# Storing each part of the last project tile once, and copying the rest during the scan

## What is computed

```python
xn = layernorm(layernorm(x)) * ln_w + ln_b
xi, z = split(xn @ W_in)                      # 512 channels each
u = silu(causal_conv(xi, 4 taps) + conv_b)
dt, Bm, Cm = split(u @ W_xproj)               # 16, 64, 64
delta = softplus(dt @ W_dt + b_dt)
for t in range(2048):                         # for each sequence, h is 512 x 64
    h = h * exp(delta[t] * A) + (delta[t] * u[t]) * Bm[t]
    y[t] = sum(h * Cm[t], over the 64 states)
out = x + layernorm(x) + ((y + u * D) * silu(z)) @ W_out
out = out + ffn(layernorm(out))               # silu(gate) * up, down
```

## Time and profile before

| what | us |
|---|---|
| median of 3 runs (lowest to highest) | 5815.9 (5814.91 to 5816.22) |
| the profiled execution | 5813.2 |
| its span | 5811.4 |
| VectorE busy in the span | 5505.2 (95%) |
| TensorE busy | 5241.6 (90%) |
| ScalarE busy | 3494.6 (60%) |
| GpSimd busy | 2262.3 (39%) |

### The profile page before, as it was taken

The page is one execution under the profiler, slowest core; times in us unless marked ns, Lnnn a source line. Parts: engine busy times, 40 slices in busy tenths (PEclk is TensorE's granted clock), DMA queues, the critical chain, the costliest instruction groups (busy, mean ns, idle before and its releaser), DMA issues. The chain is left out here.

```text
span 5811.4 us, 149606 instructions
## 1 busy us (share of the span) xinstructions
PE 5241.6 (90%) x38780; PEld 2478.7 (43%) x38780; DVE 5505.2 (95%) x3555; ACT 3494.6 (60%) x8238; POOL 2262.3 (39%) x6777
## 2 busy tenths in 40 slices
PE   5999779999999999999999999999999999997999
PEld 3344334444444444444444444444444444435666
DVE  5999989999999999999999999999999999995776
ACT  6777656666666666666666666666666666652333
POOL 2000034444444444444444444444444444440111
PEclk9999889999999999999999999999999999998999
DMA  7999942222222222222222222222222222224342
GB/s 245 332 321 337 344 111 53 54 54 55 54 52 53 54 54 54 54 52 53 54 54 55 54 52 53 54 55 54 54 52 54 53 55 54 54 44 147 115 141 73
DMA packets 1105518, 547.25 MB, mean 94 GB/s; under 512 B 753744, under 2 KB 1015056, under 8 KB 1105056
## 3 DMA queue, kind: packets, MB, share of 16 engines
q1 hardware_dynamic: 1093776, 533.89, 34.4%
q10 hardware_dynamic: 11664, 12.52, 0.6%
HBM read 296.83 MB, written 249.82 MB: 94 GB/s over the span
## 5 line engine op out<-in xcount | busy, mean ns | idle before, releaser
L997 DVE TENSOR_TENSOR_SCAN s_h<-s_decay,s_ubank 128x1024 f32<-128x1024 f32 x2048 | 4460.9, 2272 | 11.5 <-ACT s_ubank L962 11.2
L949 ACT ACTIVATE s_decay<-s_abank 128x512 f32<-128x512 f32 x4096 | 2210.4, 595 | 4.8 <-PE s_abank L887 1.4
L872 PE MATMUL s_ybank<-s_h,s_window 128*8 128x256 f32 x16416 | 1948.2, 602 | 1.9 <-DVE s_h L997 1.9
L913 PE MATMUL s_ubank<-s_x,s_w 128*128 128x256 bf16 x8192 | 1245.7, 275 | 375.5 <-DVE s_h L997 375.3
L1033 POOL TENSOR_TENSOR s_carry<-s_decay,s_h 128x64 f32<-128x64 f32 x2032 | 879.5, 433 | 1752.2 <-ACT s_decay L949 1576.4
L962 ACT ACTIVATE s_ubank<-s_seed 128x64 f32<-128x64 f32 x2048 | 478.3, 234 | 1703.2 <-PE s_ubank L913 1311.6
L887 PE MATMUL s_abank<-xnT,s_a 128*128 128x256 bf16 x8192 | 1254.9, 274 | 33.2 <-DMA s_w<-scratch_b_rows 30.1
L913 PEld LDWEIGHTS s_ubank<-s_x,s_w 128*128 128x128 bf16 x8192 | 675.7, 98 | 1197.7 <-DVE s_h L997 1096.5
L887 PEld LDWEIGHTS s_abank<-xnT,s_a 128*128 128x128 bf16 x8192 | 758.4, 98 | 195.8 <-ACT s_decay L949 35.7
L872 PEld LDWEIGHTS s_ybank<-s_h,s_window 128*8 128x8 f32 x16416 | 376.9, 97 | 839.6 <-issue 730.6
L1037 POOL TENSOR_TENSOR s_seed<-s_carry,s_first 128x64 f32<-128x64 f32 x2048 | 656.7, 321 | 164.3 <-ACT s_first L955 4.0
(11 more groups left out here) (135 smaller groups left out, 3098.2 us busy)
## 6 DMA issues: line engine op xcount, KB each, us to landing
s_x<-scratch_u_rows SPq DMA_DIRECT2D x4096, 32.0 KB
scratch_u_rows<-p_u_turn SPq DMA_DIRECT2D x90, 1024.0 KB, 6.6
scratch_delta_rows<-p_dparts SPq DMA_DIRECT2D x136, 512.0 KB, 6.2
xnT<-scratch_delta_rows SPq DMA_DIRECT2D x1024, 64.0 KB, 2.7
scratch_y<-s_y SPq DMA_DIRECT2D x1036, 16.0 KB
scratch_sz<-p_sz SPq DMA_DIRECT2D x16, 1024.0 KB, 6.2
scratch_u<-p_u SPq DMA_DIRECT2D x16, 1024.0 KB, 7.9
s_w<-scratch_b_rows SPq DMA_DIRECT2D x256, 64.0 KB, 2.4
```

The source lines that it names most:

```text
L872: last = nc.tensor.matmul(y_bank[32 * ct:32 * ct + WIN, 1 - x, :], window[:, of, (at + t) * WIN:(at + t + 1) * WIN], H[:, 1 - x, :, t], st ...
L913: last = nc.tensor.matmul(dst.rearrange("p q (a t) -> p a q t", t=2), w2[:, g, 4 * s + 2 * x + e, :], x2[:, s, :, 2 * x + e, q:q + 32, :], ...
L949: nc.scalar.activation(dst.rearrange("p x q t -> p q x t"), a_bank[:, b].rearrange("p j r (x t) -> p (j r) x t", x=2), ACT.Exp).then_inc(e ...
L997: nc.vector.tensor_tensor_scan(H[:, x, PT * p:PT * p + PT, :].rearrange("p q t -> p (q t)"), decay[:, x * (1 + c % 2), p].rearrange("p q t ...
```

## The change

In the project stage's tail, the last delta stores are cut from eight to three, one for each part, and the last u stores from five to three; the numbers that SyncE waits for are adapted. The first of COMBOS' entries, 0 to 2, are those that stay. The seven missing rows, five of delta (512 KB each) and two of u (1024 KB each), are copied from HBM to HBM by SyncE in the scan stage: one after each of the first seven groups of four chunks. For this SyncE's first 28 chunks are written out as straight code in place of loop iterations; the rest of the loop is in two pieces, from chunk 28 to 239 and from 240, and between them SyncE waits for the seven copies. Chunk 240 is the first that reads the rows of the last tile. The other engines' code is the same.

```diff
-            def back_stores(i, c, b):
+            def back_stores(i, c, b, stored=NCB):
                 sp.wait_ge(d3_done, i + 1)
-                for k, (_, j) in reversed(list(enumerate(COMBOS))):
+                for k, (_, j) in reversed(list(enumerate(COMBOS[:stored]))):
                     sp.dma_start(tile_of(d["delta_rows"][k], i), dparts[:, j]).then_inc(dparts_stored, 16)
...
-                        if j == part and k < PLACES:
+                        if j == part and k < (PARTS if last_one else PLACES):
...
             turn_stores(NT)
-            back_stores(NT, 0, BATCH)
+            back_stores(NT, 0, BATCH, PARTS)
             turn_stores(NT + 1, True)
...
-            sp.wait_ge(dparts_stored, 16 * NCB * (NT + 1))
+            sp.wait_ge(dparts_stored, 16 * (NCB * NT + PARTS))
...
-                sp.wait_ge(turns_stored[j], 16 * COPIES[j] * (NT + 3))
+                sp.wait_ge(turns_stored[j], 16 * (COPIES[j] * (NT + 2) + 1))
...
+N_COPIES = NCB - PARTS + PLACES - PARTS
+
+
+def copy_rows(eng, d, i, n, done):
+
+    if n < NCB - PARTS:
+        cols = slice(i * TW + TW, i * TW + 2 * TW)
+        eng.dma_start(d["delta_rows"][PARTS + n][:, cols], d["delta_rows"][n % PARTS][:, cols]).then_inc(done, 16)
+    else:
+        k = n - (NCB - PARTS)
+        rows = slice(i * TW + 2 * TW, i * TW + 3 * TW)
+        eng.dma_start(d["u_rows"][rows, PARTS + k, :], d["u_rows"][rows, k, :]).then_inc(done, 16)
...
-            over_chunks(sp, chunk)
+            for it in range(N_COPIES):
+                for c in range(4):
+                    chunk(it, it * 4 + c, c)
+                copy_rows(sp, d, NT - 1, it, copied)
+            last_tile = NF // 4 - NF // NT // 4
+            with sp.Fori(N_COPIES, last_tile) as it:
+                for c in range(4):
+                    chunk(it, it * 4 + c, c)
+            sp.wait_ge(copied, 16 * N_COPIES)
+            with sp.Fori(last_tile, NF // 4) as it:
+                for c in range(4):
+                    chunk(it, it * 4 + c, c)
```

More of the change, by code:

```diff
@@ L787, in scan_stage @@
         y_stored = [sem("y_stored0"), sem("y_stored1")]
+        copied = sem("s_copied")
         block = ctx.enter_context(nc.Block())
```

## The result

The changed kernel takes 5953.7 us (5948.5 to 5956.8, 6 runs) against 5815.95 us before (5814.15 to 5816.22): a ratio of 1.0238, with a 95% interval of 1.0228 to 1.0249. Forecast was 5805.0. The change is 138 us slower, not 11 us faster.

What follows compares the result with a forecast made beforehand. VectorE's scan instruction was taken to bound the scan stage, and the drain of stores to end the project stage. Gains of 9.0 + 1.9 - 0 = 10.9 us gave a forecast of 5805.0 us, range 5802.8 to 5808.5.

Steps and rivals of the forecast that it cites:

- term 3: Scan stage: the seven copies cost 0 us, since a copy may hold SyncE's load queue about 11 us before VectorE waits.
- nothing from writing out: Rival: late code fetches or transfer-bound issue in SyncE's straight chunks remove the 1.9 us gain; 5806.9 us, chance 0.13.
- with nothing to spare: Scan loop: the last x2 load's issue ends at 900.87 us and its data are used at 902.58 us.
- Term 1: Project stage's end: with fewer stores to drain, VectorE's xnT memset ends the stage; 9.0 us gained (8.8 to 9.1).
- Term 2: Scan stage's opening: written-out chunks drop SyncE's address instructions, about 0.14 us a load, plus loop entry; 1.9 us gained (0.5 to 2.3).
- the copies stop the scan: Slow-side rival: copies through one DMA engine hold up later loads, five stalls of 14 us, two of 39; 5953 us, chance 0.05.

Runs made afterwards that it cites:

- the straight run: The changed kernel with all 256 of SyncE's chunks written out and no loop at all: 5802.6 us, ratio 0.9980.
- the padded kernel: The changed kernel plus 80 no-effect SyncE instructions behind the project stage's last store and 48 between the loop's two pieces: 5806.4 us, ratio 0.9988.
- the last run: The changed kernel, all SyncE chunks written out, xnT's clearing shared by VectorE and GpSimd, which starts after VectorE's last split: 5800.8 us, ratio 0.9976.

## Why the prediction was wrong

The step that failed is the last sentence of term 3: "After the seventh copy the old loop runs with its old margins." It treats the code behind the written-out chunks as unchanged, because its instructions are. Its place is not. The sum has no term for that, and no rival had it: "nothing from writing out" looks for late fetches in the straight code, where the straight run shows none in 256 chunks, and uses the Trainium skill's rule only where it favours straight code. "Runtime: NRT & Kernel Launch" of the Trainium skill, section on instruction fetch mechanics, also says that a taken branch whose target isn't in the current window forces a fetch before execution can go on. The loop of the kernel before jumps back 63 times without the gap, which I read as that not applying here; with 32 instructions more the gap and a fetch stand at all 63 jumps. What the runs show in the step's place is a cost of 2.7 us at each of the changed kernel's 52 jumps back, 139.6 us in all, against the 0 us of the sum. The Trainium skill gives blocks of 256 instructions there and a window of two; here a shift by 128 changes nothing and one by 32 everything, so the period is no more than 128, and the measurement decides.

My own sentence on the x2 loads, "with nothing to spare", was the warning: it was used to ask what a copy may cost, not what any other delay of SyncE in the remaining 228 chunks would.

Point by point:

- *Term 1*, 9.0 us: right. 9.1 us in the two traces, 9.6 us between the medians of the run with the stores cut alone. The memset and the drain before it are as described, and the turn took 0.27 us for the 0.4 that I took; the memset starts without a stall, since its 3.36 us of "issue" stayed with less traffic, and were 1.66 us for half the size.
- *Term 2*, 1.9 us: the direction was right, the size wrong. It gives 0.4 us. The 0.5 us between the image's load and the first x1 load, which I called mostly loop entry, fell only from 0.49 to 0.40 us. The eight x1 loads still take 6.16 us (6.12 before), and two w2 loads 1.36 for 1.42: the register instructions are gone, but the issue isn't faster. I read this as full DMA engines setting the pace; no run tests it by itself. They move the same 233 GB/s in either kernel, and their share in these 6.1 us is 0.99, against 0.91 in the same stretch before (the windows of the changed kernel, then of the kernel before; the last three columns are the clock, the share and GB/s):

```profile
741.90:748.00 6.10, 0.00 (x0) 0.00 (x0) 4.93 (x4) 0.00 (x0) 2.84 (x2) 0.50 0.99 233
```

```profile
750.40:756.50 6.10, 0.00 (x0) 0.00 (x0) 4.99 (x4) 0.00 (x0) 2.79 (x2) 0.50 0.91 233
```

  Further on, the y stores save what I took (1.31 us for 1.73, 0.11 each), but the loads save less than my 0.14 us: the x1 loads take 5.30 us for 5.92, 0.08 each, and the x2 loads 5.45 for 7.25, 0.11 each. So the term was too large even where the engines have room.
- *Term 3*, 0 us: right for the copies, by a wide margin; 4.3 and 5.5 us to landing against the 11 us of room.
- *The rival on the slow side*, "the copies stop the scan", gave 5953 us and the chip shows 5954. That is a coincidence: its mechanism, a copy through one engine with 14 and 39 us of stall, isn't in the trace; no copy is waited for, and the loss comes after the last one.

With term 2 at its true size the forecast would have been 5806.5 us, and the padded kernel takes 5806.4. That close an agreement is luck. The padded kernel carries the 2.4 us of its own padding, and the kernel before, run beside it, took 5813.9 us and not 5815.9; the gain was 7.5 us, 9.9 without the padding's wait, where the corrected sum has 9.4.

## What to carry to other kernels

A change that puts instructions in front of a loop moves the loop, and on an engine whose queue has no slack that can cost more than the change is about. Look in the trace for the gap at the loop's turn and for the number of instruction fetches, before and after; a few instructions without effect tell whether it is the place, if more than one shift is tried: 128 changed nothing in either kernel, 32 did. Such padding takes time of its own, 0.067 us an instruction here, and belongs where the engine waits. Straight code, where its length is bearable, doesn't have the problem. And a wait that is removed uncovers the next: here the drain gave way to a memset some 8 us earlier, and that to the drain again after 2.6 us more.

## What the runs showed that I had not expected

- A loop of about 322 instructions on SyncE costs VectorE 2.6 us more for each jump back at one place and 4.3 us ((279.1 - 10.2) / 63) at another, with 5 fetches of 8 KB a round in both; and nothing at other places. Shifts of the kernel before by 0, 96 and 128 are fast, by 32, 64 and 160 slow. That blocks of 128 instructions are the unit, and that the limit is four blocks in place of three, is the reading that the later forecasts went by; for the four loops moved under it (the changed kernel by 80 and 48, the kernel before by 160, 64 and 96) it was right on fast or slow each time, though not on the size at 64. Which limit makes four blocks too many was not tested; no loop of another length was run.
- GpSimd's memset beside VectorE's cast of 2048 elements from f32 to bf16 came with a cast that ended 1.1 us after it (3.87 for 1.23 us), while VectorE's memset beside one of GpSimd's, in the last run, took its usual time (6.88 us and 1.66 us of issue for 8192 elements, against 13.71 and 3.36 for 16384).
